# A fused vision tower on one core: four norm factors reach channel-major form through memory, in a new order

## The chip, the core and the metric

One core of a Trainium2 chip runs the whole program: TensorE (matrix products), VectorE, ScalarE, GpSimd, and the queue of SyncE, which issues every DMA of this kernel. The metric is device time in microseconds. All data are 32-bit floats.

## The reference

Sixteen images of 64 channels and 56x56 pixels pass through three parts:

```python
t = _unfold3x3(x)                                          # 3136 tokens of 9 x 64
h1 = relu(t @ W1 + b1); s = sigmoid(h1 @ W2 + b2)
h = (t * s) @ W3 + b3                                      # plus a class token ahead
u = _layernorm(h)                                          # first layer norm
n1 = rmsnorm(u, w_norm1)                                   # w * u * rsqrt(mean(u*u) + 1e-6)
a = u + linear_attention(n1)                               # q, k: elu + 1; 8 heads
h = h + a + rmsnorm(a, w_norm2)
y = _layernorm(h)                                          # second layer norm
h = h + mixture_of_experts(y)                              # 6 experts, best 2 of a router
```

Both layer norms and both rms norms need, for each token, one factor 1/sqrt(mean over 64 channels + eps). The kernel folds the first layer norm and the first rms norm into two factors of the same variance, so there are four factors per token: u and hn (first part, "a"), b (the rms norm of the second part) and c (the second layer norm).

## The kernel before

Channels lie on partitions: two images of 64 channels fill the 128 partitions, and a block is 8 rows of 56 pixels, 448 tokens of each of the two images. 8 pairs of images of 7 blocks give 56 blocks, and a small block (8 tokens) for the class tokens. Each engine runs through the same list of steps (`for step in STEPS`), an order written out by hand for each engine: in one step block s passes the unfold part, block s-1 or s-2 the queries and keys, block s-8 the attention, s-9 the norms b and c and the router, s-10 the experts, s-11 the output. Only semaphores tie the engines together, and every engine works strictly in its order. In the first eight steps there is no second part yet, in the last ones no first part.

The parts of a block, with the lines of the profile: w1 (L324, its last part L328), relu on ScalarE, w2 in five parts (L352, L356) with tanh (L701) and the product with the pixels on VectorE (L941, gate_pixels), w3 in five parts (L368, L371); center_a (L400), squares on ScalarE, transposes to token-major form (var_mean_a, L379), q_prod (L416), kv_prod (L443), kv_outer (L455); attention (L482), att_channels (L386), out_proj (L508), mean_sq_b (L379), center_b (L523), var_mean_b (L379), router (L545), logits (L559); 21 small VectorE operations for the gates, gates_channels (L570), a copy by ScalarE, then through memory: save_gates writes 12 rows (L263), spread_gates reads them back for 64 partitions each (L274); expert_h1 (L594), expert_h2 (L614), expert_bias (L622), the gate products on VectorE (L1270), expert_out (L631), result (L1279), out_tokens (L647).

A norm factor now comes about like this: TensorE transposes the squares, VectorE sums over channels (L946) and scales, GpSimd raises to the power -0.5 (L877: one value for each token and image, 112 partitions x 8). To multiply the channel-major block by it, VectorE copies each value 64 times along the free axis (`spread_copy`, L951, to rx_u, rx_h, rx_b, rx_c), and TensorE transposes the copy in four pieces into PSUM (`to_channels`, L386). VectorE then multiplies (normed_u, normed_hn, rms_normed, normed_b).

TensorE has weights of 64 rows and 64 columns in some products. Image 0 then uses rows and columns 0-63 and image 1 rows and columns 64-127 (center_a, q_prod, out_proj), or each the other half of the columns (w1's, w2's and w3's last parts).

## Time and profile before

| | |
|---|---|
| median of three runs | 2068.82 us (2064.14 to 2079.31) |
| profiled execution | 2064.24 us, span 2062.5 us |
| TensorE | 1929.0 us busy, 94% |
| VectorE, ScalarE, GpSimd | 1295.1, 1086.0, 499.9 us busy |
| DMA | 168.31 MB, 82 GB/s on the mean |

In the rows below, "busy" of TensorE is modelled and overlapping records are merged; a group's record lasts to the end of its last product, which overlaps the next group's start. The time from one group's start to the next one's is what the group costs in sequence. "SPq" is the issuing of a DMA, not its movement.

### The profile page before, as it was taken

Reading aid. Unit: us, or ns where it says so; the run is one execution under the profiler, and the core shown is the slowest. Engines: PE = TensorE matmul, PEld = TensorE weight load, DVE = VectorE, ACT = ScalarE, POOL = GpSimd, SP = SyncE. Lnnn points to the kernel's source line nnn. Section 1 sums busy time; section 2 is a strip of 40 time slices with the busy share of each in tenths; the row PEclk is TensorE's granted clock in tenths of the full one; section 3 lists DMA queues with packets and bytes.
Section 4 is the critical chain, followed back from the end, with each engine's and each line's share of the span. In section 5 each row is a group of like instructions: output and inputs, shape, how many; then the busy total and the mean of one; then the engine's idle time right before and its main releaser. Section 6 shows DMA issues by size and latency. Waiting matters only on the chain.

```text
span 2062.5 us, 38206 instructions
## 1 busy us (share of the span) xinstructions
PE 1929.0 (94%) x13033; PEld 809.1 (39%) x13033; DVE 1295.1 (63%) x3687; ACT 1086.0 (53%) x2213; POOL 499.9 (24%) x346
## 2 busy tenths in 40 slices
PE   7888999999999999999999999999999999977775
PEld 2333344434444443444444444444444434333332
DVE  3455667576767676766667666767576767654553
ACT  3443555555555555555565655555555555543333
POOL 0112222222222222222222222222222222222120
PEclk9999999999999999999999999999999999978887
DMA  3121242424242423333333424242424232223222
GB/s 114 69 77 51 54 110 59 115 58 115 58 115 65 108 84 89 89 85 95 78 101 72 108 65 112 61 115 58 115 60 114 74 99 73 49 64 64 59 50 61
DMA packets 77184, 168.31 MB, mean 82 GB/s; under 512 B 6048, under 2 KB 62272, under 8 KB 76992
## 3 DMA queue, kind: packets, MB, share of 16 engines
q1 hardware_dynamic: 76992, 165.87, 31.0%
q8 instruction: 105, 1.72, 0.4%
q14 instruction: 87, 0.71, 0.1%
HBM read 151.80 MB, written 14.05 MB: 80 GB/s over the span
## 4 chain that ended last, share of the span: by engine, by line
issue 70%; POOL 19%; PE 8%; ACT 1%; DMA 1%; DVE 1%; POOLq 0%; SPq 0%; ACTq 0%; DVEq 0%
POOL rstd_b L877 4%; POOL rms_b L877 4%; POOL rstd_h L877 4%; POOL sum_b L899 3%; POOL h L915 3%; PE ps L352 2%; PE ps L324 2%; PE ps L368 1%; PE ps L386 0%; ACT th L701 0%; DMA gate_sp<-gates_d 0%; PE ps L371 0%; PE ps L400 0%; PE ps L443 0%; PE ps L631 0%
## 5 line engine op out<-in xcount | busy, mean ns | idle before, releaser
L701 ACT ACTIVATE th<-ps,b_half 128x448 f32<-128x448 f32 x504 | 300.5, 635 | 294.8 <-PE ps L352 247.3
L941 DVE SCALAR_TENSOR_TENSOR gated<-th,x_tile 128x448 f32<-128x448 f32 x504 | 307.6, 621 | 63.8 <-ACT th L701 37.7
L352 PE MATMUL ps<-h,packed 64*128 64x448 f32 x896 | 226.9, 582 | 30.9 <-ACT f L830 16.3
L1270 DVE TENSOR_TENSOR gh<-f,gate_sp 128x448 f32<-128x448 f32 (+1 forms) x342 | 190.6, 612 | 101.1 <-DMA gate_sp<-gates_d 88.5
L820 ACT ACTIVATE f<-ps,packed 128x448 f32<-128x448 f32 (+1 forms) x342 | 196.4, 627 | 107.5 <-PE ps L594 107.5
L830 ACT ACTIVATE f<-ps,packed 128x448 f32<-128x448 f32 (+1 forms) x342 | 201.6, 634 | 84.0 <-DVE gh L1270 82.8
L368 PE MATMUL ps<-gated,w_half 128*64 128x448 f32 x896 | 207.0, 562 | 0.0
L877 POOL TENSOR_TENSOR rstd_u<-var_u,exponent 112x8 f32<-112x8 f32 (+1 forms) x57 | 92.3, 1619 | 468.9 <-DVE var_u L967 468.9
L324 PE MATMUL ps<-x_tile,packed 128*64 128x448 f32 x896 | 185.2, 555 | 8.6 <-DMA x_tile<-x_rows 7.0
L594 PE MATMUL ps<-y,packed 64*128 64x448 f32 (+1 forms) x684 | 182.1, 610 | 2.9 <-ACT f L820 2.4
L946 DVE TENSOR_REDUCE sums_c<-ps 112x8 f32<-112x512 f32 (+1 forms) x57 | 39.0, 684 | 225.6 <-PE ps L379 225.6
L614 PE MATMUL ps<-f,packed 64*64 64x448 f32 (+1 forms) x1368 | 164.7, 551 | 9.4 <-ACT f L830 9.3
L631 PE MATMUL ps<-gh,packed 128*64 128x448 f32 (+1 forms) x684 | 163.9, 591 | 6.8 <-DVE gh L1270 6.5
L877 POOL TENSOR_TENSOR rms_b<-ms_b,exponent 112x8 f32<-112x8 f32 (+1 forms) x57 | 92.9, 1630 | 297.2 <-DVE ms_b L1123 297.2
L877 POOL TENSOR_TENSOR rstd_b<-var_b,exponent 112x8 f32<-112x8 f32 (+1 forms) x57 | 92.9, 1630 | 258.8 <-DVE var_b L1150 258.8
L899 POOL TENSOR_TENSOR sum_b<-ring,h 128x448 f32<-128x448 f32 x56 | 67.6, 1208 | 361.3 <-DVE h L1113 361.3
L718 ACT ACTIVATE xc_a<-ps 128x448 f32<-128x448 f32 (+1 forms) x57 | 30.6, 537 | 208.7 <-PE ps L400 208.7
L352 PEld LDWEIGHTS ps<-h,packed 64*128 64x128 f32 x896 | 69.8, 187 | 147.7 <-ACT th L701 58.2
L324 PEld LDWEIGHTS ps<-x_tile,packed 128*64 128x64 f32 x896 | 61.8, 139 | 98.0 <-issue 97.8
L915 POOL TENSOR_TENSOR h<-nrm_b,sum_b 128x448 f32<-128x448 f32 (+1 forms) x57 | 63.5, 1114 | 143.3 <-DVE nrm_b L1140 143.3
L877 POOL TENSOR_TENSOR rstd_h<-var_h,exponent 112x8 f32<-112x8 f32 (+1 forms) x57 | 92.3, 1619 | 0.0
L368 PEld LDWEIGHTS ps<-gated,w_half 128*64 128x64 f32 x896 | 49.5, 136 | 104.5 <-issue 62.4
(140 smaller groups left out, 3036.5 us busy)
## 6 DMA issues: line engine op xcount, KB each, us to landing
gate_sp<-gates_d SPq DMA_DIRECT2D x112, 672.0 KB, 7.6
x_tile<-x_rows SPq DMA_DIRECT2D x56, 696.0 KB, 5.4
x_tile<-x_rows SPq DMA_DIRECT2D x56, 580.0 KB, 3.9
out<-out_t SPq DMA_DIRECT2D x56, 224.0 KB, 5.2
gates_d<-gates_c SPq DMA_DIRECT2D x56, 21.0 KB
packed<-pack SPq DMA_DIRECT2D x1, 682.0 KB, 9.3
packed<-pack SPq DMA_DIRECT2D x1, 448.0 KB, 5.9
packed<-pack SPq DMA_DIRECT2D x1, 366.0 KB, 3.0
```

The lines of the kernel that those rows point to most:

```text
L324: pe.matmul(as_rows(bank(L0, p0=64 * img, p1=64 * img + 64)), cst("w1", m * C, (m + 1) * C), x_view(s, 2 * m + img), start=(m == 0), stop= ...
L352: pe.matmul(bank(S0 + img), cst("w2", m * P, (m + 1) * P)[half(img)], h1[half(img), :], start=True, stop=True).then_inc(s_done, 1)
L368: pe.matmul(bank(L0, p0=64 * img, p1=64 * img + 64), w3_half[:, m * C:(m + 1) * C], gated[u % 4][:, :], start=(m == 0), stop=False).then_i ...
L594: pe.matmul(bank(L0 + img, n), cst("ew1", ep * P, (ep + 1) * P)[half(img)], y[f % 2][half(img), 0:n], start=True, stop=True).then_inc(fh1_ ...
L614: pe.matmul(ps[col, S0 + img, 0:n], cst("ew2", ep * C, (ep + 1) * C)[half(top)], f1[(2 * ep + img) % 4][half(top), 0:n], start=True, stop= ...
L631: pe.matmul(bank(M0, n, 64 * img, 64 * img + 64), cst("ew3", j * C, (j + 1) * C), gh[j % 4][:, 0:n], start=False, stop=(ep == 2)).then_inc ...
L701: act.activation(th[(u + s) % 4][:, :], bank(S0 + u % 2), ACT.Tanh, bias=b2_half[:, m:m + 1], scale=0.5).then_inc(th_set, 1)
L820: act.activation(f1[j % 4][:, 0:n], bank(L0 + j % 2, n), ACT.Relu, bias=cst("eb1")[:, j // 2:j // 2 + 1]).then_inc(f1_set, 1)
L830: act.activation(f2[j % 4][:, 0:n], bank(S0 + j % 2, n), ACT.Relu, bias=cst("eb2")[:, j:j + 1]).then_inc(f2_set, 1)
L877: return pool.tensor_tensor(dst[0:tw, 0:n], src[0:tw, 0:n], exponent[0:tw, 0:n], ALU.pow)
L941: dve.scalar_tensor_tensor(as_rows(gated[u % 4][:, :]), as_rows(th[(u + s) % 4][:, :]), 1.0, x_view(s, u), ALU.add, ALU.mult).then_inc(gat ...
L1270: dve.tensor_tensor(gh[j % 4][:, 0:n], f2[j % 4][:, 0:n], gate_sp[:, j % 2 * (E // 2) + j // 2, 0:n], ALU.mult).then_inc(gh_set, 1)
```

## The change

The four copies by VectorE and the four groups of transposes by TensorE are gone, and with them rx_u, rx_h, rx_b and rx_c. GpSimd writes u and hn side by side into rstd_a. The SyncE queue saves the factors to six small arrays in memory and reads each back as a row, broadcast to 64 partitions, one read for each image. The sums are written in the order image, piece, so that a row in memory is in token order.

```diff
+            def save_norm(dram, src, groups, tw, done):
+                sp.dma_start(dram[0:groups * TILE].rearrange("(g p) -> p g", p=TILE)[0:tw, :],
+                             src[0:tw, 0:groups], allow_slow_non_contiguous=True).then_inc(done, 16)
+            def spread_norm(dst, dram, at, nt, tw, done):
+                rows = dram[at:at + 2 * nt * TILE].rearrange("(m x) -> m x", m=2)[:, 0:nt * tw]
+                for img in range(2):
+                    sp.dma_start(dst[half(img), 0:nt * tw],
+                                 rows[img:img + 1, :].to_broadcast([C, nt * tw])).then_inc(done, 16)
+            def save_a(r):
...
+                sp.wait_ge(rstdu_set, r + 1)
+                sp.wait_ge(rstdh_set, r + 1)
...
+                save_norm(norm_d[r % 2], rstd_a, 4 * NT if r else 2 * NT + 2, tw, na_saved)
+            def spread_a(r):
...
+                sp.wait_ge(na_saved, 16 * (r + 1))
...
+                spread_norm(rs_u, norm_d[r % 2], 0, nt, tw, ru_loaded)
...
+                spread_norm(rs_h, norm_d[r % 2], 2 * NT * TILE, nt, tw, rh_loaded)
...
-            def spread_u(r):
-                pe.wait_ge(rxu_set, r + 1)
-                to_channels(L1, rx_u, a_size(r)).then_inc(rxu_done, 1)
...
                 pe.wait_ge(kf_set, 2 * r + 2)
-                pe.wait_ge(hn_set, r + 1)
+                pe.wait_ge(qf_set, r + 1)
...
                 if 1 <= t - 1:
-                    pe.wait_ge(y_set, t - 1)
+                    pe.wait_ge(sumc_done, t - 1)
...
-                dve.tensor_reduce(dst[0:tw, 0:2 * nt], ps[0:tw, b, 0:nt * P].rearrange("p (g c) -> p g c", c=C),
+                dve.tensor_reduce(dst[0:tw, 0:2 * nt].rearrange("p (m k) -> p k m", m=2),
+                                  ps[0:tw, b, 0:nt * P].rearrange("p (k m c) -> p k m c", m=2, c=C),
...
-                dve.wait_ge(rxu_done, r + 1)
+                dve.wait_ge(ru_loaded, 32 * (r + 1))
...
-                dve.tensor_tensor(u_a[:, 0:n], xc_a[:, 0:n], bank(L1, n), ALU.mult).then_inc(u_set, 1)
+                dve.tensor_tensor(u_a[:, 0:n], xc_a[:, 0:n], rs_u[:, 0:n], ALU.mult).then_inc(u_set, 1)
...
-                if 0 <= step - 2 <= BLOCKS: q_prod(step - 2); kv_prod(step - 2)
+                if 0 <= step - 2 <= BLOCKS: kv_prod(step - 2); q_prod(step - 2)
```

save_b, spread_b, save_c and spread_c have the form of save_a and spread_a, with one array of 112 x 8 values each. The step lists of all five engines are written anew.

On TensorE, from gates_channels (ps<-packed,g_all) on. Before (rx_b is norm b's factor; f_0 to f_3 are expert hidden values; sq_b to sq_c squares for the variances):

```order
L570 MATMUL ps<-packed,g_all 12x112 x4
L371 MATMUL ps<-gated,w_half 64x448 x2
L455 MATMUL ps<-v_tok,k_tok 64x65 x8
L647 MATMUL ps<-packed,res 112x128 x4
L594 MATMUL ps<-y,packed 128x448 x2
L482 MATMUL ps<-kv_m,ring 112x72 x8
L386 MATMUL ps<-packed,rx_b 128x112 x4
L594 MATMUL ps<-y,packed 128x448 x2
L614 MATMUL ps<-f_0,packed 64x448 x2
L614 MATMUL ps<-f_1,packed 64x448 x2
L523 MATMUL ps<-h_0,packed 64x448 x2
```

And of the change, from the same place:

```order
L623 MATMUL ps<-packed,g_all 12x112 x4
L647 MATMUL ps<-y,packed 128x448 x2
L667 MATMUL ps<-f_0,packed 64x448 x2
L667 MATMUL ps<-f_1,packed 64x448 x2
L580 MATMUL ps<-h_0,packed 64x448 x2
L647 MATMUL ps<-y,packed 128x448 x2
L543 MATMUL ps<-kv_m,ring 112x72 x8
L451 MATMUL ps<-packed,sq_c 112x128 x4
L472 MATMUL ps<-ring,packed 64x448 x2
L396 MATMUL ps<-x_tile,packed 64x448 x2
```

The last part of w3 (before L371), kv_outer (L455), out_tokens (L647) and the first expert_h1 (L594) have moved ahead of gates_channels; center_a (after L472) stands right behind the variance of c.

On TensorE further on, of the change: w1's last part (L400) with out_proj (L569), up to expert_out (L684).

```order
L451 MATMUL ps<-packed,sq_a 112x128 x4
L458 MATMUL ps<-packed,att 128x112 x4
L396 MATMUL ps<-x_tile,packed 64x448 x6
L400 MATMUL ps<-x_tile,packed 64x448 x2
L569 MATMUL ps<-att_c,packed 64x448 x2
L667 MATMUL ps<-f_0,packed 64x448 x2
L667 MATMUL ps<-f_1,packed 64x448 x2
L675 MATMUL ps<-gates_c,packed 128x448
L684 MATMUL ps<-gh,packed 64x448 x2
```

Out_proj stood with q_prod before; it now follows w1's last part, where center_a stood (there L400, before w1's L328).

On TensorE, of the change, around kv_prod (L504) and q_prod (L483):

```order
L440 MATMUL ps<-gated,w_half 64x448 x4
L424 MATMUL ps<-h,packed 128x448 x2
L504 MATMUL ps<-wkv_n,u_a 112x128 x8
L483 MATMUL ps<-u_a,wq_n 64x448 x2
L428 MATMUL ps<-h,packed 64x448 x2
L440 MATMUL ps<-gated,w_half 64x448 x4
L443 MATMUL ps<-gated,w_half 64x448 x2
L516 MATMUL ps<-v_tok,k_tok 64x65 x8
```

Q_prod now comes after kv_prod and is followed by w2's last part (L428); before, out_proj, q_prod and kv_prod followed each other. Three parts of w2 and w3 that came after kv_prod now come ahead of it.

The queue of SyncE, one step of it. Before:

```order
L255 DMA x_tile<-x_rows 128x1160 [waits w1_done,gated_set]
L255 DMA x_tile<-x_rows 128x1392
L263 DMA gates_d<-gates_c 12x448 [waits gate_loaded,gatesc_set]
L287 DMA out<-out_t 112x2x256 [waits outt_set]
L274 DMA gate_sp<-gates_d 64x6x448 [waits gh_set,gate_saved]
L274 DMA gate_sp<-gates_d 64x6x448
```

Of the change, from the gates' read to the next step's save of the gates:

```order
L341 DMA gate_sp<-gates_d 64x6x448
L260 DMA norm_d<-rstd_b 112x8x1 [waits rc_loaded,rstdb_set]
L260 DMA norm_d<-rstd_a 112x16x1 [waits ru_loaded,rh_loaded,rstdh_set,rstdu_set]
L267 DMA rs_c<-norm_d 64x448 [waits y_set,nc_saved]
L267 DMA rs_c<-norm_d 64x448
L267 DMA rs_u<-norm_d 64x448 [waits u_set,na_saved]
L267 DMA rs_u<-norm_d 64x448
L267 DMA rs_h<-norm_d 64x448 [waits hn_set]
L267 DMA rs_h<-norm_d 64x448
L260 DMA norm_d<-rms_b 112x8x1 [waits rb_loaded,rmsb_set]
L267 DMA rs_b<-norm_d 64x448 [waits nrm_set,nb_saved]
L267 DMA rs_b<-norm_d 64x448
```

Behind these stand the store of the output, the save of the gates, the x load and the read of the gates, in this order; the x load stood ahead of the save of the gates before.

## Rows read from the trace of the kernel before

**Rows 1.** Windows: start:end, length, busy of PE, PEld, DVE, ACT, POOL; clock, DMA, GB/s.

```profile
67.00:101.00 34.00, 28.97 (x188) 11.18 (x184) 15.82 (x36) 14.18 (x28) 6.47 (x4) 1.00 0.22 77
...
1000.00:1760.00 760.00, 748.48 (x5208) 315.54 (x5208) 508.62 (x1455) 433.74 (x880) 200.07 (x136) 1.00 0.34 88
...
1854.00:2000.00 146.00, 111.80 (x630) 47.52 (x629) 76.56 (x225) 55.35 (x109) 27.77 (x20) 0.81 0.27 57
```

**Rows 2.** Timeline of the SyncE queue, middle of the run: start, duration, line, transfer.

```profile
1004.57 0.83 SPq L255 DMA_DIRECT2D x_tile<-x_rows  x2
1005.50 0.34 SPq L263 DMA_DIRECT2D gates_d<-gates_c  x1
...
1010.46 1.25 SPq L274 DMA_DIRECT2D gate_sp<-gates_d  x2
1038.27 0.83 SPq L255 DMA_DIRECT2D x_tile<-x_rows  x2
```

**Rows 3.** The same timeline in the last steps.

```profile
1868.93 0.31 SPq L263 DMA_DIRECT2D gates_d<-gates_c  x1
...
1870.43 1.25 SPq L274 DMA_DIRECT2D gate_sp<-gates_d  x2
1896.33 0.31 SPq L263 DMA_DIRECT2D gates_d<-gates_c  x1
```

**Rows 4.** Timeline of TensorE, 1003 to 1028 us: start, duration, line, operands, records.

```profile
1003.89 0.55 PE L386 MATMUL ps<-packed,rx_h 112*128 112x112 f32 x4
1004.27 0.55 PE L570 MATMUL ps<-packed,g_all 112*12 112x112 f32 x4
1004.75 0.97 PE L371 MATMUL ps<-gated,w_half 64*64 64x448 f32 x4
...
1007.89 1.01 PE L482 MATMUL ps<-kv_m,ring 64*112 64x72 f32 x16
1008.83 0.60 PE L386 MATMUL ps<-packed,rx_b 112*128 112x112 f32 x4
1009.36 1.02 PE L594 MATMUL ps<-y,packed 64*128 64x448 f32 x4
...
1014.17 0.65 PE L379 MATMUL ps<-packed,sq_c 128*112 128x128 f32 x4
...
1017.91 0.59 PE L400 MATMUL ps<-ring,packed 64*64 64x448 f32 x2
1017.92 0.59 PE L328 MATMUL ps<-x_tile,packed 64*64 64x448 f32 x2
...
1018.71 0.93 PE L614 MATMUL ps<-f,packed 64*64 64x448 f32 x8
...
1020.52 0.60 PE L386 MATMUL ps<-packed,rx_c 112*128 112x112 f32 x4
1020.96 0.60 PE L379 MATMUL ps<-packed,sq_a 128*112 128x128 f32 x4
1021.49 0.97 PE L631 MATMUL ps<-gh,packed 128*64 128x448 f32 x4
...
1026.92 0.60 PE L386 MATMUL ps<-packed,rx_u 112*128 112x112 f32 x4
1027.36 0.55 PE L386 MATMUL ps<-packed,att 112*128 112x112 f32 x4
```

**Rows 5.** DMA busy tenths, 1000 to 1034 us in 40 slices; VectorE's first gate products.

```profile
DMA  0000007699892089999996000000000000000000
...
1019.76 2.23 DVE L1270 TENSOR_TENSOR gh<-f,gate_sp 128x448 f32<-128x448 f32 x4 [1.82 <-DMA gate_sp<-gates_d]
```

**Rows 6.** The DMA queue over the span; DMA issues, the last block's (KB each, us to landing).

```profile
q1 hardware_dynamic: 76992, 165.87, 31.0%
...
gate_sp<-gates_d SPq DMA_DIRECT2D x2, 12.0 KB, 2.4
```

**Rows 7.** Timeline of GpSimd: the power for norm c's factor.

```profile
1015.84 1.65 POOL L877 TENSOR_TENSOR rstd_b<-var_b,exponent 112x8 f32<-112x8 f32 x1 [4.48 <-DVE var_b L1150]
```

More of the change, by code:

```diff
@@ L108, in build @@
         var_h = sb("var_h", [TILE, 2 * NT])
-        rstd_u = sb("rstd_u", [TILE, 2 * NT])
-        rstd_h = sb("rstd_h", [TILE, 2 * NT])
-        rx_u = sb("rx_u", [TILE, NT * P])
-        rx_h = sb("rx_h", [TILE, NT * P])
+        rstd_a = sb("rstd_a", [TILE, 4 * NT])
+        rs_u = sb("rs_u", [P, N])
+        rs_h = sb("rs_h", [P, N])
+        rs_b = sb("rs_b", [P, N])
+        rs_c = sb("rs_c", [P, N])
         eq = sb("eq", [P, N])
@@ L133, in build @@
         rms_b = sb("rms_b", [TILE, 2 * NT])
-        rx_b = sb("rx_b", [TILE, NT * P])
         sum_b = sb("sum_b", [P, N])
@@ new lines, in save_b, with spread_b @@
+            def save_b(t):
+                nt, tw = b_size(t)
+                sp.wait_ge(rmsb_set, t)
+                if 32 * (t - 2) > 0:
+                    sp.wait_ge(rb_loaded, 32 * (t - 2))
+                save_norm(norm_d[2 + t % 2], rms_b, 2 * nt, tw, nb_saved)
+            def spread_b(t):
+                nt, tw = b_size(t)
+                sp.wait_ge(nb_saved, 16 * t)
+                if t - 1 > 0:
+                    sp.wait_ge(nrm_set, t - 1)
+                spread_norm(rs_b, norm_d[2 + t % 2], 0, nt, tw, rb_loaded)
@@ new lines, in save_c, with spread_c @@
+            def save_c(t):
+                nt, tw = b_size(t)
+                sp.wait_ge(rstdb_set, t)
+                if 32 * (t - 2) > 0:
+                    sp.wait_ge(rc_loaded, 32 * (t - 2))
+                save_norm(norm_d[4 + t % 2], rstd_b, 2 * nt, tw, nc_saved)
+            def spread_c(t):
+                nt, tw = b_size(t)
+                sp.wait_ge(nc_saved, 16 * t)
+                if t - 1 > 0:
+                    sp.wait_ge(y_set, t - 1)
+                spread_norm(rs_c, norm_d[4 + t % 2], 0, nt, tw, rc_loaded)
@@ L299, in _ @@
             for step in STEPS:
[L300 to L303 removed]
+                if 0 <= step - 4 <= BLOCKS: spread_a(step - 4)
+                if 1 <= step - 11 <= CLS_T: save_b(step - 11); spread_b(step - 11)
+                if 1 <= step - 15 <= CLS_T: store_out(step - 15)
+                if 1 <= step - 12 <= CLS_T: save_gates(step - 12)
+                if 3 <= step - 1 <= BLOCKS: load_x(step - 1)
+                if 1 <= step - 12 <= CLS_T: spread_gates(step - 12)
+                if 1 <= step - 11 <= CLS_T: save_c(step - 11)
+                if 0 <= step - 3 <= BLOCKS: save_a(step - 3)
+                if 1 <= step - 11 <= CLS_T: spread_c(step - 11)
             sp.wait_ge(out_stored[0], 16 * (CLS_T // 2))
@@ L650, in _ @@
             pe.wait_ge(pack_loaded[0], 16)
-            pe.wait_ge(setup_dve, 3)
+            pe.wait_ge(setup_dve, 4)
             for step in STEPS:
+                if 1 <= step - 11 <= CLS_T: gates_channels(step - 11); expert_h1(step - 11, 1); expert_h2(step - 11, 0)
+                if 1 <= step - 10 <= CLS_T: center_b(step - 10)
+                if 1 <= step - 11 <= CLS_T: expert_h1(step - 11, 2)
+                if 1 <= step - 9 <= BLOCKS: attention(step - 9)
+                if 1 <= step - 10 <= CLS_T: var_mean_b(step - 10)
+                if 0 <= step - 2 <= BLOCKS: center_a(step - 2)
+                if 1 <= step - 1 <= BLOCKS: w1(step - 1, 0)
+                if 1 <= step - 11 <= CLS_T: expert_h2(step - 11, 1)
+                if 0 <= step - 2 <= BLOCKS: var_mean_a(step - 2)
+                if 1 <= step - 9 <= BLOCKS: att_channels(step - 9)
+                if 1 <= step - 1 <= BLOCKS: w1(step - 1, 1); w1(step - 1, 2); w1(step - 1, 3); w1(step - 1, 4)
@@ L657, in _ @@
+                if 1 <= step - 1 <= BLOCKS: w2(step - 1, 1)
                 if 1 <= step - 9 <= CLS_T: mean_sq_b(step - 9)
-                if 0 <= step - 2 <= BLOCKS: spread_hn(step - 2)
-                if 1 <= step - 10 <= CLS_T: gates_channels(step - 10)
-                if 1 <= step - 1 <= BLOCKS: w3(step - 1, 4)
+                if 1 <= step - 10 <= CLS_T: router(step - 10)
+                if 1 <= step - 1 <= BLOCKS: w2(step - 1, 2)
+                if 1 <= step - 10 <= CLS_T: logits(step - 10)
@@ L679, in _ @@
-                if 1 <= step <= BLOCKS: w2(step, 1)
-                if 1 <= step - 9 <= CLS_T: router(step - 9)
-                if 0 <= step - 1 <= BLOCKS: spread_u(step - 1)
-                if 1 <= step - 8 <= BLOCKS: att_channels(step - 8)
-                if 1 <= step - 9 <= CLS_T: logits(step - 9)
-                if 1 <= step <= BLOCKS: w3(step, 0); w2(step, 2)
         @block.scalar
@@ L1425 @@
     gates_d = [nc.dram_tensor(f"gates_d{k}", (2 * E, N), F32, kind="Internal").ap() for k in range(2)]
-    build(nc, ap_x, ap_p, gates_d, ap_o)
+    norm_d = [nc.dram_tensor(f"norm_d{k}", (4 * NT * TILE,), F32, kind="Internal").ap() for k in range(6)]
+    build(nc, ap_x, ap_p, gates_d, norm_d, ap_o)
     r = run_bass_kernel_spmd(nc, [{"x_rows": x_rows, "pack": pack}], core_ids=[0])
```

237 lines of the change are left out of this document (93 added, 144 removed).

## The prediction

> **What bounds the kernel now.** I read the busy time by windows first. Between 1000 and 1760 us TensorE is busy 748.48 of 760 us at full granted clock [rows 1]; ScalarE, VectorE and GpSimd are busy for a third to two thirds of it. The store-and-load queue issues the x load once per step, at 1004.57 and at 1038.27 us, so a step is 33.70 us [rows 2], and TensorE's idle share of it is 11.52 / 760 x 33.7 = 0.5 us. The middle of the run is TensorE's work laid end to end, so what leaves TensorE there counts in full until something else ends last. The last ten steps are different: TensorE is busy 111.80 of 146 us at clock 0.81, and the gate saves stand 1896.33 - 1868.93 = 27.40 us apart [rows 1, 3]. There a chain of waits sets the pace. The first eight steps have only the unfold and query side; TensorE is busy 28.97 of 34 us [rows 1].
>
> **What leaves TensorE.** Each to-channels group is priced from its start to the next group's start, which takes pipelining into account: rx_h 4.27 - 3.89 = 0.38 us, rx_b 9.36 - 8.83 = 0.53, rx_c 20.96 - 20.52 = 0.44, rx_u 27.36 - 26.92 = 0.44 (all + 1000) [rows 4]. Sum 1.79 us per step.
>
> **What the order changes on TensorE.** In the step now, center_a (L400) and the last part of w1 (L328) use the two opposite pairs of 64x64 quarters of the array; their records interleave and both together take 18.71 - 17.91 = 0.80 us [rows 4]. A group of that size alone lasts 0.97 us (L371, 4.75), of which I count 0.9 in sequence [rows 4]. The new order has this kind of neighbours twice: w1's last part with out_proj, and q_prod with w2's last part; center_a stands alone. One pair more is worth 0.9 us per step. TensorE without waits is then 33.70 - 0.5 - 1.79 - 0.9 = 30.5 us per step.
>
> **The gates come late.** Before, gates_channels starts at 1004.27 and expert_out at 1021.49: 17.2 us of TensorE work lie between [rows 4]. After, w3's last part, kv_outer, out_tokens and expert_h1(0) are no longer there (7.89 - 4.75 = 3.14 us), nor rx_b and rx_c (0.97), nor an idle 0.2; center_a alone and att_channels come in (0.9 + 0.5). That leaves 14.3 us. Meanwhile the gates still travel through memory. Now gate_sp is awaited by VectorE until 1019.76, that is 15.5 us after gates_channels began [rows 5]. The DMA strip shows the x load and store until about 1010.4, a gap, and the gate rows from 1011.6 to 1018.4 [rows 5]. After, the save goes out first, 1.1 us after gates_channels starts (as now: 5.50 - 4.27 = 1.23 [rows 2]); x follows at once and is moving from 2.4 for 4.4 us (the strip has 5.0 for x and the store); the save has landed in 1.5 us (1868.93 to 1870.43 [rows 3]), so the gate rows wait in the queue behind x and the gap closes. They move from 6.9 to 13.5 and are seen at about 14.5, 1.0 us better than now. Two gate products (half of 2.23 us [rows 5]) put expert_out at 15.7, against 14.3 of TensorE work: 1.4 us of stall. VectorE comes out of this wait with six gate products, the residual, two pixel gates, normed_b and the result in a row; by the residual between the fourth and fifth product and by the result before the router I count 0.4 us more. At the step's end the last tanh waits behind the exponentials of k and q, and the pixel gate for w3's last part is ready some 0.35 us late. Step after: 30.5 + 1.4 + 0.4 + 0.35 = 32.65 us, 1.05 less than now.
>
> **The norm factors' round trip.** A copy and four transposes become a save of single floats and two broadcast reads. The trace has no save of single floats. Count of pieces: 16 x 112 = 1,792 for the a pair, 896 each for b and c. Issue: a 12-row save takes 0.34 us of the queue, two gate reads of 384 pieces 1.25 us [rows 2], so 0.75 us per 1,000 pieces as the low bound. Movement: the last block's gate read has 384 pieces of 32 B and lands in 2.4 us [rows 6]; the high bound is the mean packet of the whole queue, 31.0% of 16 engines x 2062.5 us / 76992 = 0.13 us [rows 6]. On 16 engines 1,792 pieces are 112 each: 2.4 / 384 x 1792 = 11 us if even the fixed latency scaled, 15 us at the high bound, 1 to 3 us if a small piece goes as fast as issue. I take 3.0 us for issue and movement of the a save, 1.5 for b and c, each with 1.5 us to land, since size is what a small piece lacks and the 2.4 us are mostly latency. The Trainium skill (DMA: Bandwidth & Descriptors, Rules for kernel authors) speaks against the change: a strided last dimension becomes one descriptor per element, and it says to rearrange instead. By its table's floor of about 10.5 ns per packet (same page, Bandwidth) the a save would move in some 1.2 us, an estimate that leaves my sum as it is; its warning, taken as a slow save, is the slower rival below.
>
> Is there room? For c: the transposes start at 1014.17 and the power ends at 1017.49, 3.3 us [rows 4, 7]; after, they start at 5.1, so save_c goes out at 8.4, but behind the gate rows, which move until 13.5; it lands at about 15. The queue is then in save_a (variance at 8.9, reduction, two powers of 1.65 us [rows 7]: from 13.1 to 16.1), so the c reads go out at 16.1 and land at about 19.2. VectorE comes to normed_b at 19.8. Hidden, by 0.6 us only. For u: the reads land at about 20.5, normed_u is due at 23. For b: save at 23.5, reads landed at 30, due at 32.7. VectorE loses four copies, which are off the path. Reading the factors from SBUF in place of PSUM I count at nothing.
>
> **Start and end.** In the first eight steps the a round trip (about 7.5 us) replaces a copy and transposes (about 1), but three pairs of w2 and w3 have been put ahead of kv_prod; I count no change there, and +4.5 us a step at the most. In the last steps no x load competes: gates seen at 11.4, normed_b before 16, result at 17, router, logits and the gate arithmetic to 24. So 24 us in place of 27.4, for 9 steps: 30 us. I take 28.
>
> **Sum.** 47 steps with both sides x 1.05 = 49; with the end, 77. The profiled execution took 2064.2 us (span 2062.5); it becomes 1987. The median of the three runs is 4.6 us above it: 1992 us.
>
> **Rivals.**
> - The forecast (0.45): 1992 us, 1970 to 2020 by the bounds on the gate wait of 1.0 to 2.0 us.
> - TensorE is never kept waiting by the gates (0.12), if x and the gate rows together move faster. Steps of 30.85: 47 x 2.85 + 28 = 162 less, 1907 us. Against it: the strip shows the engines full while they move.
> - The extra pair does not overlap (0.08), because w2's last part waits for tanh. Then 0.9 x 47 = 42 more: 2034 us.
> - A norm factor is a little late (0.15): 1 to 2 us a step are lost and the steps stay near 33.7, 2040 to 2080 us. The room of 0.6 us for c speaks for it.
> - Slower (0.20): the saves of single floats are slow. Place: the queue in save_c and save_a, with the c reads behind both. It decides from where the two saves take 1.6 us more than my 4.5 us, 0.6 of room and 1.05 of gain, about 36 ns per piece and engine. At 60 ns (6.7 + 3.4 us) the c reads come 5.0 us too late and the step grows to 37.7: 47 x 4.0 = 188 more, and the end gains nothing, near 2250 us. At the high bound (22 us for both) the step reaches 50 us.
>
> **How the numbers follow.** A difference under about 1% can't be told from none here. Faster by over 1% (under 2048): 0.45 + 0.12 + 0.08 + a third of 0.15 = 0.70. Same: 0.10. Slower: 0.20. Range: from the fast rival to the slightly late one, 1900 to 2080 us, leaves the slow saves out.
>
> **What would show it.** Right: no to-channels groups but att; TensorE's idle time mostly ahead of expert_out (L684), released by the gate products and these by gate_sp; the records of q_prod and w2's last part interleaved; steps near 32.7 us and end steps near 24. Wrong: VectorE waiting long for rs_c, rs_b or rs_u; the queue busy for more than 3 us in one save; steps above 33.7 us; a granted clock below 1.0 in the middle.

## The result, and the profile after

The changed kernel takes 2739.2 us (median of four runs, 2726.1 to 2752.0); the kernel before takes 2074.1 us beside it. The ratio is 1.323, with a 95% interval of 1.314 to 1.331. I had predicted 1992 us and a range of 1900 to 2080: the wrong sign, and far outside. It is the slower rival that came, at its high end. Two of the four runs of one kernel below, that with runs of four floats, fell into a slower state at a lower granted clock, and its time is that of the other two.

The changed kernel's page gives the busy time, the clock and the packets. The last two lines of this fence are groups of instructions: busy time and mean ns of one, then the idle time before them and what ended it.

```profile
PE 2037.0 (75%) x12133; PEld 806.6 (30%) x12133; DVE 1291.2 (47%) x3460; ACT 1093.5 (40%) x2213; POOL 542.3 (20%) x346
...
PEclk9888898888888888888888888888888888877676
...
DMA packets 317189, 220.46 MB, mean 81 GB/s; under 512 B 217384, under 2 KB 302280, under 8 KB 317000
...
L684 PE MATMUL ps<-gh,packed 128*64 128x448 f32 (+1 forms) x684 | 208.6, 729 | 188.5 <-DVE gh L1283 188.4
...
L598 PE MATMUL ps<-y,packed 64*32 64x224 f32 (+1 forms) x452 | 47.5, 500 | 300.2 <-DVE res L1292 291.7
```

The middle window of [rows 1] at the same times (columns as there):

```profile
1000.00:1760.00 760.00, 589.37 (x3630) 235.71 (x3630) 383.48 (x1023) 324.82 (x656) 166.16 (x102) 0.87 0.45 87
```

In the middle TensorE was busy 748 of 760 us at clock 1.00; now it is busy 589 at 0.87. It stands still before the router (L598) and before expert_out (L684), 489 us together. The router's wait is put down to `res`, but `res` stands behind y on VectorE, and y waits for the factor of c. VectorE's own waits, and those of the queue that issues the transfers (who waits <- for what: us in all, times, longest):

```profile
DVE y L1182 <- DMA rs_c<-norm_d: 332.3, 56, 11.6
```

```profile
SPq L267 <- DMA norm_d<-rstd_b: 450.2, 57, 12.0
SPq L267 <- DMA norm_d<-rms_b: 375.4, 57, 7.4
...
SPq L267 <- DMA norm_d<-rstd_a: 239.5, 54, 9.0
```

For 1065 us of 2730 the queue stands still until a save of factors has landed. One step of it, as the timeline of the SyncE queue shows it (start, duration of the issue, line, transfer):

```profile
1414.60 0.31 SPq L260 DMA_DIRECT2D norm_d<-rms_b  x1
1421.48 1.08 SPq L267 DMA_DIRECT2D rs_b<-norm_d  x2
...
1428.99 1.34 SPq L341 DMA_DIRECT2D gate_sp<-gates_d  x2
1434.76 0.33 SPq L260 DMA_DIRECT2D norm_d<-rstd_b  x1
1439.76 0.33 SPq L260 DMA_DIRECT2D norm_d<-rstd_a  x1
1452.20 1.11 SPq L267 DMA_DIRECT2D rs_c<-norm_d  x2
```

The save of b, 896 single floats with nothing else under way, takes 6.9 us to the issue of its reads (14.60 to 21.48). The save of c, behind the gate rows and with the save of a beside it, takes 17.4 us. In the first steps, where only a's 1,792 floats travel, a save takes 7.8 us, and the steps are 27.2 us long (the next save of a is issued at 89.48):

```profile
62.28 0.33 SPq L260 DMA_DIRECT2D norm_d<-rstd_a  x1
70.03 1.09 SPq L267 DMA_DIRECT2D rs_u<-norm_d  x2
```

Where do the 665 us come from? GpSimd's sum_b comes once a step, and 44 middle steps lie between its records at 325.41 and 2320.65 us: 45.35 us each. Before it was 33.75 (256.92 to 1742.05 for the same 44). That is 11.6 us x 47 = 545. The nine steps behind them take 35.8 instead of 27.9 each, 71 more (the last six of them 34.9 instead of 27.0), and the first sum_b comes at 237.8 instead of 190.3, 48 more.

### The profile page after: what moved, and what is told of

The parts are those of the page before. It is cut to its first block and busy times, and to the rows that moved or that the text cites. A ratio compares the mean times of both kernels' runs of the same rounds, so it can differ in the third digit from the quotient of the medians.

```text
span 2730.1 us, 36915 instructions
## 1 busy us (share of the span) xinstructions
PE 2037.0 (75%) x12133; PEld 806.6 (30%) x12133; DVE 1291.2 (47%) x3460; ACT 1093.5 (40%) x2213; POOL 542.3 (20%) x346
## 5 line engine op out<-in xcount | busy, mean ns | idle before, releaser
L986 DVE SCALAR_TENSOR_TENSOR gated<-th,x_tile 128x448 f32<-128x448 f32 x504 | 342.2, 709 | 176.8 <-ACT th L748 141.7
L684 PE MATMUL ps<-gh,packed 128*64 128x448 f32 (+1 forms) x684 | 208.6, 729 | 188.5 <-DVE gh L1283 188.4
L424 PE MATMUL ps<-h,packed 64*128 64x448 f32 x896 | 295.7, 744 | 35.3 <-ACT th L748 22.5
L598 PE MATMUL ps<-y,packed 64*32 64x224 f32 (+1 forms) x452 | 47.5, 500 | 300.2 <-DVE res L1292 291.7
L440 PE MATMUL ps<-gated,w_half 128*64 128x448 f32 x896 | 250.6, 691 | 0.2 <-DVE gated L986 0.2
L647 PE MATMUL ps<-y,packed 64*128 64x448 f32 (+1 forms) x684 | 193.5, 643 | 28.5 <-DVE kv_sum L1076 19.9
L1182 DVE TENSOR_TENSOR y<-xc_b,rs_c 128x448 f32<-128x448 f32 (+1 forms) x57 | 35.2, 617 | 332.3 <-DMA rs_c<-norm_d 332.3
L836 ACT ACTIVATE rh<-ps,packed 128x224 f32<-128x224 f32 (+1 forms) x57 | 25.3, 444 | 358.2 <-PE ps L598 358.2
L922 POOL TENSOR_TENSOR rstd_a<-var_u,exponent 112x8 f32<-112x8 f32 (+1 forms) x57 | 92.4, 1621 | 283.8 <-DVE var_u L1008 283.8
L684 PEld LDWEIGHTS ps<-gh,packed 128*64 128x64 f32 x684 | 49.9, 177 | 334.0 <-DVE gh L1283 290.5
L1102 DVE TENSOR_SCALAR den<-ps 112x32 f32<-112x32 f32 x112 | 21.0, 188 | 243.0 <-PE ps L543 243.0
```

The source lines that it names most:

```text
L424: pe.matmul(bank(S0 + img), cst("w2", m * P, (m + 1) * P)[half(img)], h1[half(img), :], start=True, stop=True).then_inc(s_done, 1)
L440: pe.matmul(bank(L0, p0=64 * img, p1=64 * img + 64), w3_half[:, m * C:(m + 1) * C], gated[u % 4][:, :], start=(m == 0), stop=False).then_i ...
L647: pe.matmul(bank(L0 + img, n), cst("ew1", ep * P, (ep + 1) * P)[half(img)], y[f % 2][half(img), 0:n], start=True, stop=True).then_inc(fh1_ ...
L684: pe.matmul(bank(M0, n, 64 * img, 64 * img + 64), cst("ew3", j * C, (j + 1) * C), gh[j % 4][:, 0:n], start=False, stop=(ep == 2)).then_inc ...
L922: return pool.tensor_tensor(dst[0:tw, 0:n], src[0:tw, 0:n], exponent[0:tw, 0:n], ALU.pow)
L986: dve.scalar_tensor_tensor(as_rows(gated[u % 4][:, :]), as_rows(th[(u + s) % 4][:, :]), 1.0, x_view(s, u), ALU.add, ALU.mult).then_inc(gat ...
```

## The experiments

### Saves alone

A program of saves, each issued when the one before has landed; it computes nothing of the reference.

```
dma(d[0:8*112].rearrange("(g p) -> p g"), src[0:112, 0:8])   # also 16, 4, 2 groups
dma(d[0:8*112].rearrange("(p g) -> p g"), src[0:112, 0:8])   # rows of eight floats
dma(d.rearrange("(g p s) -> p g s", s=16)[:, :, 0], ...)     # 64 B apart (s=128: 512 B)
dma(d.rearrange("(p g s) -> p g s", s=2)[:, :, 0], ...)      # 8 B apart, a stretch per partition
```

> This kernel computes nothing: it only issues single transfers, each five times, and waits for each before the next, so the gap between two issues is the whole cost of one. Forms: 112 partitions x 16, 8, 4 and 2 single floats to memory with the floats of a partition 448 B apart (1792, 896, 448, 224 pieces); 112 rows of 8 floats together; 896 single floats 8 B apart, each partition in its own stretch; the same 64 B apart and 512 B apart; 8 rows of 112 floats; the 896 floats read back as single floats; a row of 448 floats read by 64 partitions; 12 rows of 448 floats. In the changed kernel a save of 896 single floats with nothing beside it took 6.9 us to the next issue and one of 1792 took 7.8. Theory A (the memory side handles each small write slowly, whatever its address): 896 pieces take about 6.9 us in all address forms, 224 pieces near 3, rows of 8 floats about 2. Theory B (small writes to the same short stretch of memory from several engines hold each other up): 896 pieces take 6.9 us in the form of the kernel, but about 2 us when 512 B apart, and the form in which each partition has its own stretch is fast too. Theory C (it is the number of pieces on the reading side or in the issue): the read back as single floats is as slow as the save.

Windows over five saves of one form each (start:end, length; the last three numbers are the clock, the busy share of the DMA engines and GB/s), in this order: 16, 8 and 2 groups of 112 single floats side by side (the window of 4 groups is left out, and that of 512 B), rows of eight, a stretch per partition, 64 B apart.

```profile
1.42:39.07 37.65, 0.00 (x0) 0.00 (x0) 1.00 0.12 1
39.07:73.97 34.90, 0.00 (x0) 0.00 (x0) 1.00 0.06 1
...
108.54:143.54 35.00, 0.00 (x0) 0.00 (x0) 1.00 0.02 0
143.54:150.39 6.85, 0.00 (x0) 0.00 (x0) 1.00 0.05 3
150.39:178.96 28.57, 0.00 (x0) 0.00 (x0) 1.00 0.08 1
178.96:190.04 11.08, 0.00 (x0) 0.00 (x0) 1.00 0.20 2
```

A fifth of the lengths: 7.5, 7.0 and 7.0 us for 1792, 896 and 224 single floats. The number of pieces does not matter. What matters is where they lie: the same 896 floats 64 B apart take 2.2 us, and rows of eight 1.4 us. Theory B comes nearest, but it had the stretch per partition fast, and that form takes 5.7 us; theory C falls, as 896 single floats are read back in 2.1 us each time (207.47 to 217.84 for five).

While the slow saves run the DMA engines are busy for 2 to 12% of the time. The first save of 1,792 floats (issued at 1.42) and the first of 896 (issued at 39.07) show when:

```profile
2.25:3.55 1.30, 0.00 (x0) 0.00 (x0) 1.00 0.68 6
...
39.87:40.67 0.80, 0.00 (x0) 0.00 (x0) 1.00 0.55 5
40.67:45.76 5.09, 0.00 (x0) 0.00 (x0) 1.00 0.00 0
```

The engines move the 896 floats between 0.8 and 1.6 us after the issue. Then nothing moves for 5.1 us before the save is seen to have landed; with 1,792 floats it is 1.3 us of movement and 5.5 us of nothing (3.55 to 9.10). So it is not the engines that are slow: what is long is the time between the last movement and the landing. Every price per piece in my prediction asked the wrong question.

### Saves of rows in the whole kernel

```diff
-                sp.dma_start(dram[...].rearrange("(g p) -> p g", p=TILE)[0:tw, :],
+                order = "(p g) -> p g" if tw == TILE and done in (na_saved, nb_saved, nc_saved) else "(g p) -> p g"
+                sp.dma_start(dram[...].rearrange(order, p=TILE)[0:tw, :],
```

> The changed kernel with one edit: the saves of full blocks write the 8 or 16 floats of a partition together (112 pieces in place of 896 or 1792), so the factors come back in the wrong token order; every other operation, wait and transfer is the same. Theory A (single-float saves that land late, and hold up what is behind them in the queue, are the cause): saves land in about 1.5 to 2 us, VectorE no longer waits for rs_c, the granted clock returns to 1.0 in the middle, a step takes 32 to 34 us and the whole 1980 to 2060 us. Rival (the round trip through one in-order queue with 11 more transfers a step is too long in any form): the saves get cheaper but the c reads stay behind save_a and the gate rows, steps of 38 us or more, above 2300 us. Rival (the new order itself costs the time): steps stay near 46 us, above 2600 us.

2091.6 us, ratio 1.014 (1.010 to 1.018), above the 1980 to 2060 that theory A gave, and far below both rivals. Of the 665 us, 648 go. The step is 34.27 us (267.74 to 1775.83 for 44), and a save of b takes what it takes alone, 1.4 us to the issue of its reads (1022.62 to 1023.99).

So the saves of single floats are the cause of the slowdown. But cheap saves do not bring my 1992 us either: 100 us of the forecast were wrong for other reasons. The longest of TensorE's waits in this kernel is the one before expert_out:

```profile
PE ps L685 <- DVE gh L1284: 50.1, 55, 3.1
```

Ahead of expert_h1(0) it waits 19.9 us more for VectorE's kv_sum, 0.4 us a step.

### Rows for the factor of c alone

```diff
-  ... done in (na_saved, nb_saved, nc_saved) ...
+  ... done in (nc_saved,) ...
```

> The changed kernel, where only the save of norm c writes its 8 floats of a partition together (wrong token order for c alone); a and b stay single floats. If the c save alone, and what it does to the gate rows ahead of it, is the cause, most of the loss is gone: the gate rows are seen some 3 us earlier, the c reads 10 us earlier, and the kernel takes 2150 to 2300 us. If every single-float save holds the queue, the c reads still wait for the a save that is issued before them, and b's round trip still takes 7 us before its read: above 2400 us.

2377.8 us (one run), step 38.70 us: between the two cases expected, so neither fits. The save of c is worth about 361 us, 6.6 us a middle step, and those of a and b together about 286 us, 4.4 us a step. So c's save costs on the path, and so do the other two beside it; a and b were not tried apart. The waits on the queue for these two go on:

```profile
SPq L268 <- DMA norm_d<-rms_b: 343.4, 57, 7.0
SPq L268 <- DMA norm_d<-rstd_a: 290.8, 55, 7.9
```

### The pair of q_prod and w2

The kernel with rows, and q_prod ahead of kv_prod, so that it no longer stands beside w2's last part.

```diff
-                if 0 <= step - 2 <= BLOCKS: kv_prod(step - 2); q_prod(step - 2)
+                if 0 <= step - 2 <= BLOCKS: q_prod(step - 2); kv_prod(step - 2)
```

> The kernel with the floats saved in rows (e_rows) with q_prod ahead of kv_prod again, so that w2's last part has kv_prod ahead of it and does not overlap with q_prod. If the overlap of products on opposite quarters is worth 0.9 us a step where TensorE is the bound, this is 40 us slower than e_rows; if w2's last part waits for tanh anyway, or if TensorE isn't the bound, the two agree within 10 us.

2120.2 us (one run): the pair is worth about 29 us, and 0.55 us a middle step (34.82 against 34.27), not the 0.9 (42 us) that I counted. In the kernel with rows the records of the two overlap by half only (timeline of TensorE), w2's last part starting 0.44 us after q_prod:

```profile
1025.35 0.97 PE L484 MATMUL ps<-u_a,wq_n 64*64 64x448 f32 x4
1025.79 0.97 PE L429 MATMUL ps<-h,packed 64*64 64x448 f32 x4
```

### How far apart is far enough

A second program of saves and reads; again it computes nothing of the reference.

> A program of saves alone, each issued when the one before has landed, five of each form; it computes nothing of the reference. In the first such program 224, 448, 896 and 1792 single floats that lie next to each other in memory all took about 7 us (6.9 to 7.5), rows of eight floats 1.4 us, and 896 single floats 64 bytes apart 2.2 us. Theory (single floats that fall into one 64-byte stretch hold each other up, their number does not matter): 896 floats 4 and 16 bytes apart 6 to 7 us, 32 bytes apart in between or slow, 64 bytes apart 2.2 us; runs of 8 floats 1.4 us; runs of 2 floats slow like single ones. Rival (a run under 32 bytes is slow by itself, wherever it lies): contradicted already by the 64-byte pitch, so it would have to show runs of 2 and 4 floats at 2.2 us. Two saves of single floats under way together: about 7 us for both if they wait on themselves, about 14 if they share one slow place. A spread read with a save of single floats behind it: its own completion comes at 2.8 us if the later save does not touch it, and several us later if it does.

Windows of five saves each, columns as above: 896 single floats 4, 16 and 32 B apart (64 B, which takes as long as 32, is left out); then 896 floats in adjacent runs of two and four (eight, 1.4 us as in the program before, is left out); then pairs of saves of single floats under way together.

```profile
3.62:39.06 35.44, 3.18 (x5) 0.00 (x0) 1.00 0.06 1
39.06:53.12 14.06, 0.00 (x0) 0.00 (x0) 1.00 0.16 1
53.12:65.83 12.71, 0.00 (x0) 0.00 (x0) 1.00 0.17 1
...
78.51:97.47 18.96, 0.00 (x0) 0.00 (x0) 1.00 0.06 1
97.47:110.35 12.88, 0.00 (x0) 0.00 (x0) 1.00 0.05 1
...
117.18:157.52 40.34, 0.00 (x0) 0.00 (x0) 1.00 0.11 1
```

7.1, 2.8 and 2.5 us; 3.8 and 2.6 us; 8.1 us for two together. (VectorE's products in the first window belong to the last point of this document.) My theory named the wrong size: 16 B apart is enough, I had said 64. In the forms tried, what holds a save up is several small pieces inside one 16-byte stretch: four of them 7 us, two of them 3.8 us as runs (5.7 as single floats of one partition in the program before), one 2.5 to 2.8 (2.2 for 64 B apart in the program before). The rival, that a small run is slow wherever it lies, falls too. Two saves together take little more than one, so neither waits for the other to be through. A read with such a save issued right behind it was seen after 2.7 to 3.7 us, alone after 2.7 to 3.2: that does not explain gates that come 3.5 us late.

### The same number of pieces, 64 B apart, in the whole kernel

```diff
-                sp.dma_start(dram[0:groups * TILE].rearrange("(g p) -> p g", p=TILE)[0:tw, :],
+                    out_ap = dram[0:groups * TILE * 16].rearrange("(g p s) -> p g s", p=TILE, s=16)[0:tw, :, 0]
```

> The changed kernel, but each factor is written as a single float 64 bytes from its neighbour (same number of pieces, same order of the steps; the reads are as they were, so the factors read are not the right ones; six small writes are added at the start). Theory (the saves are slow because single floats share a 64-byte stretch of memory): about 2091 us like the kernel that saves rows, at most 2125 since such a save takes 2.2 us alone instead of 1.4. Rival (the number of pieces is what costs, 1792 and twice 896 a step): about 2739 us, as the changed kernel.

2118.7 us, ratio 1.026 (1.023 to 1.029), step 34.76, as forecast. This settles it: as many pieces as in the changed kernel, and 620 us less. The queue waits 110 us for the saves of b, where it waited 375:

```profile
SPq L271 <- DMA norm_d<-rms_b: 109.7, 57, 2.9
```

### Rows, with the gate rows ahead of x

```diff
-                if 3 <= step - 1 <= BLOCKS: load_x(step - 1)
                 if 1 <= step - 12 <= CLS_T: spread_gates(step - 12)
+                if 3 <= step - 1 <= BLOCKS: load_x(step - 1)
```

> The kernel that saves the factors in rows, with one more edit: SP issues the two reads of the gate rows before the load of x instead of behind it (factors in the wrong token order, as there). Theory (what is left of the loss is that the gates come late: TensorE idle 1.2 us a step in front of expert_out): 2091.6 - 47 x 1.2 = 2035 us, and the gates seen about 12 us instead of 14.4 us after gates_channels. Rival (x then comes late instead, or the wait before expert_out moves to the next factor): 2080 to 2110 us.

2071.2 us, ratio 1.001 (0.999 to 1.004). Of the wait before expert_out 6.8 us are left of 50.1, but of the 56 us forecast only 20 came, because another wait opened, as the rival had it; it stands before the router, where it was 3.5 us in the kernel with rows:

```profile
PE ps L599 <- DVE res L1293: 64.8, 55, 2.0
```

The timeline of the queue shows why:

```profile
991.29 1.27 SPq L256 DMA_DIRECT2D x_tile<-x_rows  x2
995.70 0.33 SPq L261 DMA_DIRECT2D norm_d<-rstd_b  x1
...
1003.64 1.11 SPq L268 DMA_DIRECT2D rs_c<-norm_d  x2
```

The reads of c go out 8 us after its save, and 2.6 us after the queue was done with the save of a (1000.70 to 1001.03). A save that takes 1.4 us alone had not been seen to land before, with 1.3 MB of gate rows and as much of x issued ahead of it.

### Correct factors from runs of four floats

The squares go to the tile so that a partition's four tokens are neighbours, and a save writes runs of 16 B; the reads stay as they are. The gate rows are ahead of x.

```diff
+                    d, a = d.rearrange("(q p k) -> p q k", p=TILE, k=NT), a.rearrange("p (q k) -> p q k", k=NT)
...
-                act.activation(sq_a[:, 0:n], bank(L1, n), ACT.Square).then_inc(sqa_set, 1)
+                act.activation(by_group(sq_a[:, 0:n], nt), by_token(bank(L1, n), nt), ACT.Square).then_inc(sqa_set, 1)
```

> The whole computation again, with factors in their right places: the squares are written so that the token-major tile holds tokens in runs of four, a save then writes runs of four floats (16 bytes) instead of single floats, the reads stay whole rows, and SP issues the reads of the gate rows before the load of x. Theory (single floats side by side are slow, runs of 16 bytes are not: 2.4 us alone against 7.0 and, for rows of eight, 1.4): the time of the kernel that saves rows with the gates first, 2071 us, plus up to 1 us a step for the slower save of c, 2071 to 2118. Rival (16-byte runs share 64-byte stretches like single floats do and are slow when the queue is full): 2400 us or more.

2139.4 us (2131.2 and 2147.6) against 2071.9 before, a ratio of 1.03: 21 us above the theory's 2118 and far below the rival's 2400, with 600 us less than the changed kernel. The wait before the router grew from 64.8 to 101.5 us, which is 37 of the 68 us that this kernel takes more than the one before; the rest was not traced. The squares of b, which ScalarE now reads from SBUF in strides of 16 B, take 1.03 us in place of 0.58; the squares read from PSUM cost nothing more (538 ns). The timeline of ScalarE:

```profile
1012.93 1.03 ACT L821 ACTIVATE sq_b<-h 128x448 f32<-128x448 f32 x1 [0.44 <-DVE h L1150]
```

TensorE's wait ahead of the router:

```profile
PE ps L608 <- DVE res L1302: 101.5, 54, 4.1
```

### Gates and x through ScalarE's queue

```diff
                 if 1 <= step - 11 <= CLS_T: out_copy(step - 11)
+                if 1 <= step - 10 <= CLS_T: save_gates(step - 10)
                 if 1 <= step - 10 <= CLS_T: relu1(step - 10, 2); relu1(step - 10, 3)
+                if 1 <= step - 10 <= CLS_T: spread_gates(step - 10)
+                if 3 <= step + 1 <= BLOCKS: load_x(step + 1)
```

> v_runs, but ScalarE issues the save and the two reads of the gate rows and the two loads of x, so that they go through another queue than the saves and reads of the factors. Theory (with rows or runs what is left of the loss is that a small save waits in SP's queue behind the bytes of gate rows and x: the factors of c are seen 7 to 8 us after their save is issued where a save alone takes 1.4, and TensorE's router waits 1.4 us a step for y and res): the router's wait goes, 2071 - 47 x 1.4 = 2005 us, up to 2050 as ScalarE now spends 2 to 3 us a step on issuing. Rival (the DMA engines are shared whichever queue is used, or ScalarE becomes late): 2070 to 2150 us.

2142.7 us, ratio 1.034 (1.028 to 1.040), as the rival had it: the queue apart gained nothing on the 2139.4. The router's wait falls from 101.5 to 26.8 us, but ScalarE now does the issuing in its own order, and xc_b behind it is late (ACTq is ScalarE's issuing side):

```profile
1019.62 1.29 ACTq L904 DMA_DIRECT2D gate_sp<-gates_d  x2
1021.00 1.07 ACTq L885 DMA_DIRECT2D x_tile<-x_rows  x2
1022.17 0.55 ACT L806 ACTIVATE xc_b<-ps 128x448 f32<-128x448 f32 x1 [2.25 <-issue]
```

ScalarE's last activation ends at 1019.91, when the first of these issues has already begun. So the save of the gates had landed by then, and the 2.25 us are the four issues themselves (so in 10 of the 11 steps from 900 to 1300 us); the next forecast, which puts them down to the landing, reads this wrongly. TensorE stands 61.7 us for the squares behind xc_b.

### The issues moved to other places

The reads of the gate rows behind square_c, x ahead of hidden; the squares of b in order again, and their transposes take every fourth column.

```diff
                 if 1 <= step - 9 <= CLS_T: center_b(step - 9); square_c(step - 9)
+                if 1 <= step - 10 <= CLS_T: spread_gates(step - 10)
...
+                if 3 <= step + 1 <= BLOCKS: load_x(step + 1)
                 if 1 <= step <= BLOCKS: hidden(step)
```

> v_queue with three places changed: ScalarE issues the reads of the gate rows only after square_c (in v_queue it stood still 2.5 us a step there, waiting for the gate rows' save to land), it issues the load of x before hidden, and the squares of b are written in order again and picked up in runs of four by the transposes (ScalarE took 1.03 us for them against 0.58). Theory (what v_queue lost is ScalarE's wait, 22 us in 600 in front of the transposes of sq_c, and the router's wait is really gone, 8 us in 600 against 32): 2142.7 - 1.3 x 47 = 2082 us, less 0.4 us a step for the squares of b: 2060 to 2085. Rival (the gates now come late again, 2 us later than with v_runs): 2120 to 2150 us.

2099.9 us, ratio 1.015 (1.012 to 1.018), 15 us above the forecast's range. One more edit lets TensorE transpose the output between kv_outer and expert_h1(0):

```diff
-                if 1 <= step - 10 <= CLS_T: expert_h1(step - 10, 0)
                 if 1 <= step - 11 <= CLS_T: out_tokens(step - 11)
+                if 1 <= step - 10 <= CLS_T: expert_h1(step - 10, 0)
```

> v_q2, and TensorE transposes the output between kv_outer and the first expert_h1 instead of behind it, where it waits 0.42 us a step for VectorE's sum_kv. Theory (a wait in TensorE's own order is worth its length): v_q2 - 47 x 0.42 = 20 us less than v_q2. Rival (other waits close the loop, the gates or the factor of c): within 5 us of v_q2.

2100.9 us, 1.014 (1.011 to 1.017): no gain. The wait of 0.42 us a step for kv_sum is gone, but the same products now wait 22.5 us in all for ScalarE's f, against 8.6 before. What else stood in front of TensorE:

```profile
PE ps L459 <- ACT f L858: 34.2, 43, 1.8
PE ps L589 <- DVE res L1317: 26.4, 45, 2.0
```

center_a (L459) waits for ScalarE, which is late by its two issues of gate rows, and the router (L589) still waits for c, whose reads now travel beside x and are seen after 4.2 us; in the kernel with rows it was 2.8.

### x at the end of ScalarE's step, gates on the sync queue

```diff
                 if 1 <= step <= BLOCKS: gate_tanh(step, 0); gate_tanh(step, 1); gate_tanh(step, 2); gate_tanh(step, 3)
+                if 3 <= step + 1 <= BLOCKS: load_x(step + 1)
```

> v_q2_out with the gate rows back on SP (ahead of everything but their own save) and only the two loads of x issued by ScalarE, at the end of its step behind the fourth gate_tanh, where it waits for TensorE in any case. Theory (three waits of v_q2_out come from ScalarE's issues and from x in the wrong place: 13 us in 600 in front of center_a, 10 before the router, and the read of c's factor takes 5.2 us beside x against 3): about 1.2 us a step less than v_q2_out, 2100.9 - 56 = 2045 us, under the 2071 of the kernel before. Rival (the middle step of about 33.5 us is held by something else than these waits, since every version with fast saves shows it, whatever was moved): 2085 to 2105 us.

2028.4 us, ratio 0.983 (0.981 to 0.986), 17 us better than forecast: faster than the changed kernel and, by 1.7%, than the one before, with the whole computation done. TensorE is busy again and at full clock, the step is 32.69 us (262.83 to 1701.11 for 44), and the router's wait, the second fence, is nearly gone:

```profile
1000.00:1600.00 600.00, 573.97 (x3949) 233.09 (x3948) 419.46 (x1117) 354.69 (x713) 181.03 (x111) 1.00 0.48 120
```

```profile
PE ps L611 <- DVE res L1317: 7.0, 13, 2.1
```

The Trainium skill (DMA: Bandwidth & Descriptors, Rules for kernel authors) says that spreading transfers over issuing engines brings no bandwidth, as all use the same 16 engines. The runs agree as far as they go: with gates and x on ScalarE's queue nothing was gained at first (2142.7 against 2139.4 us). This last kernel changed two things: the gate rows are back on the sync queue, and x moves at another time. It is issued at 1012.47, behind the reads of the factors of c and a (1007.16 to 1012.05), where the one before had it at 1005.89, ahead of them (1010.13). The two changes, and time and queue of x, were not tried apart.

## Why the prediction was wrong

**What bounds the kernel, what leaves TensorE: right.** The to-channels groups are gone, and TensorE is busy 554.88 of 600 us in the kernel with rows, that is 31.7 us of each step of 34.27, and 573.97 of 600 or 31.3 us in the last one. I had 30.5. The pair was mis-sized by 0.35 us (0.55 for 0.9), the clock of 0.98 stretches the first of the two numbers, and the transposes by strides add 0.05 us to the second (0.70 for 0.65 us); some 0.4 us are not traced.

**The norm factors' round trip: the step that failed.** "I take 3.0 us for issue and movement of the a save, 1.5 for b and c, each with 1.5 us to land, since size is what a small piece lacks and the 2.4 us are mostly latency." Measured: 0.31 to 0.33 us of issue, and 7.8 and 6.9 us from issue to reads. Alone, issue and movement take 2.1 us for a's 1,792 floats and 1.6 for 896, which is near my 3.0 and 1.5; it is the landing behind them, put at 1.5 us, that takes 5.1 to 5.5. The time to land, which no row had but for a save of 12 rows, is the term that failed. The low bound came from issue slopes and from pieces of 32 B [rows 2, 6], the kind that this trace shows to be fast. I chose near the low end, with a reason that no row bore out. The high bound was 22 us for the saves of a and c and a step of 50 us; c's reads went out 17.4 us after its save with the gate rows ahead and the save of a beside it, and the step is 45.3. The bound held by luck of size, since the cost does not go by pieces. The rule of the Trainium skill that I had put beside my sum (DMA: Bandwidth & Descriptors, Rules for kernel authors), to rearrange rather than to write a strided last dimension, was the better guide, and the runs agree: 2091.6 us with rows against 2739.2. The number of descriptors that it names is not what costs, as the kernel with as many pieces 64 B apart shows (2118.7 us). The estimate by the skill's floor of about 10.5 ns per packet (same page, Bandwidth), 1.2 us of movement for the save of a, is near the 1.3 us measured; the landing is not in it.

**The place: right.** "Place: the queue in save_c and save_a, with the c reads behind both." VectorE waits 332 us for rs_c, TensorE 292 us for `res` behind it.

**The gates: right where the saves are fast.** In the kernel with rows expert_out starts 15.6 us after gates_channels, forecast 15.7, and the first products come at 14.4, forecast 14.5. In the changed kernel they come at 17.9 (1426.36 to 1444.26). From 1440 to 1444 the DMA engines are 86% busy with 2 GB/s, and every packet is under 512 B, so these are floats and not gate rows:

```profile
1440.00:1444.00 4.00, 0.83 (x2) 0.11 (x1) 0.00 (x0) 0.00 (x0) 0.00 (x0) 1.00 0.86 2
...
DMA packets 1820, 0.01 MB, mean 2 GB/s; under 512 B 1820, under 2 KB 1820, under 8 KB 1820
```

So here, other than with a save alone, the floats do keep the engines busy, and the gate rows had been moved some 4 us before they were seen. Why they are seen only at the end of that stretch stays open; the read with one save behind it did not show it.

**Late factors: mis-sized.** I had c hidden by 0.6 us. With rows that holds (3.5 us of the router's wait are left), and it broke as soon as the gates came earlier. I had looked for the wait that ends last and not for the one behind it.

**The step: mis-sized.** My sum took 1.05 us a step off, and the kernel with rows adds 0.5. TensorE's work is 31.7 us where I had 30.5, and its waits are 2.6 where I had 2.15: 1.2 before expert_out (1.4 forecast), and the rest in small waits for tanh, the pixel gate, f and kv_sum. In its profiled execution (2095.0 us, 1987 forecast) the 47 middle steps are 72 us of the miss, the start 10 and the end 26.

**Start and end: wrong.** My end step had "gates seen at 11.4, normed_b before 16, result at 17", and "24 us in place of 27.4". With fast saves the last six steps take 26.4 us, before 27.0. In one of them, from gates_channels at 1926.66, the gates are seen at 12.3, normed_b comes at 17.9 and the result at 19.0, and the next gates_channels at 27.2. The products right behind gates_channels, which waits 4.2 us there, run slowly, and my chain had none that did:

```profile
1927.51 1.86 PE L648 MATMUL ps<-y,packed 64*128 64x448 f32 x4
```

At the start I counted no change, and with fast saves the first sum_b is 10 us late (200.5 for 190.3). In the changed kernel it is 48 us late, where I had allowed 4.5 us a step for eight steps, 36.

**The clock: not in the sum.** I named a clock below 1.0 as a sign, and gave it no price. TensorE's busy time is 2037 us against 1843 with rows for the same matmuls, so 194 of the 637 us between the two profiled executions are slower TensorE, and its idle time (693 against 250 us) is the rest. Behind the wait of 4.6 us before expert_out the granted clock is 0.50, the lower of its two levels, and the same group of w2 takes 1.86 us where at full clock it takes 1.02:

```profile
1446.00:1450.00 4.00, 4.00 (x12) 1.04 (x10) 2.52 (x5) 2.19 (x5) 0.00 (x0) 0.50 0.07 0
...
1447.17 1.86 PE L424 MATMUL ps<-h,packed 64*128 64x448 f32 x4
...
1451.86 1.02 PE L424 MATMUL ps<-h,packed 64*128 64x448 f32 x4
```

**The chances.** 0.20 for slow saves was too little when no row showed one and the bounds ran from 1 to 15 us. An unknown cost that stands three times a step on a path with 0.6 us of room should have carried about half. One reading of a row was also off, without weight: GpSimd is busy for 200 of 760 us, a quarter and not a third.

## What to carry to other kernels

Before a value goes through memory, look at how it lies there, not at how many pieces it has: turn the tile so that each piece is at least 16 B and, if it can be, a row. Where the one number that decides is in no row of the trace, let the range take in both of its bounds. A small transfer that others wait for should not be issued right behind megabytes (a save that lands in 1.4 us alone held its reads back for 8); move the big one to a time when nobody waits, and expect each removed wait to bring out the next. An engine that issues a transfer in its own order pays for the issue: four of them kept ScalarE from its next activation for 2.2 us.

## What the runs showed of the hardware

- A save of single floats side by side in memory takes 7.0 us for 224 of them and 7.5 for 1792, with the DMA engines 2 to 12% busy; 16 B apart 2.8 us, in rows of eight 1.4 us. For 896 floats the engines are done 1.6 us after the issue, and 5.1 us more pass before it is seen to land. What in the memory holds them is not shown.
- Issuing a save of 224 to 1792 single floats takes the queue 0.30 to 0.34 us, and 0.56 us right behind another issue.
- When GpSimd's power and two pixel gates on VectorE run at the same time, both take longer: the gates 2.09 us for 1.16 without it, and the power 1.95 for 1.65. They come from the kernel with the gate rows ahead of x:

```profile
1009.12 2.09 DVE L987 SCALAR_TENSOR_TENSOR gated<-th,x_tile 128x448 f32<-128x448 f32 x2
1009.29 1.95 POOL L923 TENSOR_TENSOR rms_b<-ms_b,exponent 112x8 f32<-112x8 f32 x1 [8.67 <-DVE ms_b L1151]
```

- VectorE's product of 128x448 takes 0.96 us with one operand in strides of 32 B in SBUF, 0.62 us without (three of each, in the second program of saves).
